# Quantised cross attention: the last two of six projection roundings moved from VectorE to ScalarE

## The reference

```python
def _fq(x, delta, zp, n_bits):
    xi = _round_ste(x / delta) + zp
    xq = jnp.clip(xi, 0.0, 2.0 ** n_bits - 1.0)
    return (xq - zp) * delta

def _attn(x, ctx, wq, wk, wv, wo, bo, dq, dk, dv, dw):
    q = (x @ wq).reshape(b, n, H, DH).transpose(0, 2, 1, 3)
    k = (ctx @ wk).reshape(b, m, H, DH).transpose(0, 2, 1, 3)
    v = (ctx @ wv).reshape(b, m, H, DH).transpose(0, 2, 1, 3)
    sim = einsum('bhid,bhjd->bhij', _fq(q, dq, 128.0, 8), _fq(k, dk, 128.0, 8)) * SCALE
    attn = jax.nn.softmax(sim, axis=-1)
    out = einsum('bhij,bhjd->bhid', _fq(attn, dw, 0.0, 8), _fq(v, dv, 128.0, 8))
    return out.transpose(0, 2, 1, 3).reshape(b, n, D) @ wo + bo
```

## Time and profile before

| | |
|---|---|
| median of 3 runs | 2308.91 us (2307.79 to 2310.9) |
| the profiled execution's own time | 2313.39 us |
| its span in the trace | 2311.7 us |
| PE / DVE / ACT / POOL busy, whole span | 1911.3 / 1630.2 / 1309.5 / 1001.5 us |
| mean granted TensorE clock, whole span | 0.912 of full |
| quantised cross attention, first to last instruction | about 1632 to 2247 us |

### The profile page before, as it was taken

How to read it: one execution, slowest core, us unless ns; L and a number is a source line. 1 busy time by engine, 2 the same in 40 slices (tenths; PEclk the granted TensorE clock), 3 DMA queues, 4 the chain that set the end, 5 groups by cost and what they waited for, 6 DMA issues and landing times. The chain is left out here.

```text
span 2311.7 us, 58368 instructions
## 1 busy us (share of the span) xinstructions
PE 1911.3 (83%) x20005; PEld 1291.4 (56%) x20005; DVE 1630.2 (71%) x2948; ACT 1309.5 (57%) x2351; POOL 1001.5 (43%) x1181
## 2 busy tenths in 40 slices
PE   4888666699999999999887777445699999999988
PEld 3887233266666666666533444223366666666653
DVE  4899597666666666666433224998499999999984
ACT  2555243366666676666533333222588888888863
POOL 2333162355455455445000000331488888888840
PEclk9999798799999999999888888555799999999999
DMA  7777000233333233333009991000111111111100
GB/s 195 247 242 234 9 1 0 64 84 94 86 86 98 82 88 98 85 94 88 21 11 282 266 256 37 0 0 0 54 42 40 40 40 40 46 47 40 40 1 16
DMA packets 64287, 190.37 MB, mean 82 GB/s; under 512 B 19886, under 2 KB 27295, under 8 KB 64223
## 3 DMA queue, kind: packets, MB, share of 16 engines
q1 hardware_dynamic: 59614, 164.95, 26.0%
q0 software_dynamic: 4608, 24.58, 2.7%
HBM read 127.13 MB, written 25.49 MB: 66 GB/s over the span
## 5 line engine op out<-in xcount | busy, mean ns | idle before, releaser
L1284 DVE TENSOR_REDUCE c_part<-c_mxp 128x1 f32<-128x500 f32 x672 | 428.8, 678 | 211.9 <-PE c_mxp L1164 211.7
L1232 ACT ACTIVATE c_e<-c_stp 125x896 f32<-125x896 f32 x384 | 349.3, 917 | 167.7 <-PE c_stp L1178 166.4
L1927 ACT ACTIVATE c_e<-c_sp,alpha 128x750 f32<-128x750 f32 x448 | 391.8, 886 | 78.3 <-PE c_sp L1872 78.0
L1164 PE MATMUL c_mxp<-c_kh,c_qb 128*128 128x500 f16 x672 | 254.5, 381 | 7.2 <-DVE c_part L1284 3.7
L1963 DVE TENSOR_SCALAR c_ph<-c_e,c_inv 128x1500 f16<-128x1500 f32 x224 | 259.8, 1160 | 0.1
L1949 DVE TENSOR_SCALAR c_pt<-c_tp 125x768 bf16<-125x768 f16 x448 | 243.2, 546 | 1.0 <-PE c_tp L1885 0.2
L1885 PE MATMUL c_tp<-ident_h,c_ph 128*128 128x128 f16 x2688 | 223.8, 219 | 21.9 <-DVE c_pt L1949 21.5
L1885 PEld LDWEIGHTS c_tp<-ident_h,c_ph 128*128 128x128 f16 x2688 | 177.2, 98 | 106.2 <-DVE c_pt L1949 57.7
L1872 PE MATMUL c_sp<-c_ki,c_qb 128*128 128x375 bf16 x896 | 218.7, 326 | 12.2 <-ACT c_e L1927 11.8
L1178 PE MATMUL c_stp<-c_qs,c_ks 103*128 103x224 f16 x1536 | 210.2, 259 | 2.5 <-ACT c_e L1232 2.5
L742 POOL TENSOR_TENSOR s_qb<-qi,mask_head_ 128x896 bf16<-128x896 f32 (+1 forms) x32 | 54.7, 1712 | 324.8 <-SPq L735 231.9
(11 more groups left out here) (276 smaller groups left out, 3723.3 us busy)
## 6 DMA issues: line engine op xcount, KB each, us to landing
c_ct<-ctx_turned SPq DMA_DIRECT2D x64, 750.0 KB
ctx_turned<-l_ct POOLq DMA_DIRECT2D x32, 750.0 KB, 4.1
c_ks<-c_kh SPq DMA_DIRECT2D x256, 93.8 KB
f_ct<-ctx_turned SPq DMA_DIRECT2D x32, 750.0 KB
l_cn<-in_ctx SPq DMA_DIRECT2D x32, 672.0 KB
f_cn<-in_ctx SPq DMA_DIRECT2D x32, 672.0 KB
c_ks<-c_kl SPq DMA_DIRECT2D x128, 93.8 KB
l_cn<-in_ctx SPq DMA_DIRECT2D x32, 78.0 KB
```

The source lines that it names most:

```text
L1164: pe.matmul(mxp[:, (PIECES * p + s) % 2, 0:500], qh[p][:, 128 * (s // 3):128 * (s // 3) + 128], kh[p][:, 500 * (s % 3):500 * (s % 3) + 500 ...
L1232: act.activation(e[:, j % (2 * GROUP), :].rearrange("p (a c) -> p a c", a=2), stp[0:KP, 2 * (j % 2):2 * (j % 2) + 2, 0:448], ACT.Exp, scal ...
L1284: dve.reduce_max(part[:, s // 3, s % 3:s % 3 + 1], mxp[:, (PIECES * p + s) % 2, 0:500], axis=AX.X).then_inc(piece_max, 1)
L1927: act.activation(e[t % E_BUFFERS][:, HALF * h:HALF * h + HALF] .rearrange("p (k c) -> p k c", k=2), sp_[:, 2 * h:2 * h + 2, 0:375], ACT.Ex ...
```

## The change

The table of indices that VectorE rounds becomes empty. ScalarE's loop then makes all six roundings, and VectorE's branch at L1987 never runs.

```diff
@@ -1763,7 +1763,7 @@
         WEIGH = {4: (0, 6), 6: (6, NJ)}
         TURN_LAG = 3
         E_BUFFERS = 4
-        ON_VECTOR = (4, 5)
+        ON_VECTOR = ()
         USED_BACK = [4 if t >= E_BUFFERS else NT if t == 3 else 3 for t in range(NT)]
         ct = pair("ct", [128, NK])
         ki = pair("ki", [128, NK], BF16)
```

## The result

The changed kernel takes 2293.8 us in the median of six runs (2288.55 to 2301.13), against 2309.23 us (2306.55 to 2310.9) for the kernel before. The ratio is 0.9936, with a 95% interval of 0.9921 to 0.9951: faster by 0.64%, or 15.4 us. The prediction had 2298.0 us, 10.9 us faster. One later execution of the kernel before took 5438 us at a granted clock of 0.344 and is in none of the comparisons.

A forecast was written before the change was run, and what follows sets the result against it. It took a ring of waits over several engines, not VectorE alone, as the bound. 31 batches by 0.40 us less 1.5 gave 10.9 us, so 2298.0 us from the median 2308.91, range 2276 to 2305.

The forecast's parts named there:

- the ring: Cycle of waits through POOL, VectorE and TensorE that sets the 18.43 us period; the fifth projection's rounding lies on it.
- Gain 0.40 us per period: TensorE's sixth projection no longer waits for VectorE's rounding of the fifth to empty the PSUM bank: 0.40 us per period.
- margin and schedule on ScalarE: ScalarE rounds the fifth projection from about 1962.2 to 1963.0, 0.3 us before TensorE is ready for the sixth.
- I take zero: VectorE's weights of tile 6 meet POOL's query spread; whichever starts first, POOL comes out within 0.1 us of today.
- The ring is closed: From sixth projection to weighing, whose eighth key tile releases POOL's conversion; one moved rounding lies on this path, for 0.40 us.
- Cost 1.5 us, once: Before the first batch's exponentials, the table load comes behind ScalarE's sixth rounding: 1.5 us once, bounds 0 to 3.
- The sum: 31 batches by 0.40 us less 1.5 at the start: 10.9 us faster, 2298.0 us from the median 2308.91.
- VectorE as the only bound: Rival: VectorE's time decides, both roundings count whole, 1.32 us per period, 39.4 us faster, 2269.5; chance 5%.
- The bank no freer: Rival: ScalarE's rounding ends as late as VectorE's did, only the start's cost remains, 2310.4 us; chance 10%.
- ScalarE as the ring: Rival: delayed exponentials of tile 6 hold up POOL's total, 9.6 us slower, 2318.5 us; chance 6%.
- POOL's chain shortening: Rival: VectorE's weights of tile 6 leave POOL's way, saving a further 0.68 us per period, 2277 us; chance 7%.
- The signs named: Trace signs: period 18.03 us, sixth projection without wait, POOL waiting near 0.9; wrong if the period is below 17.9.

The follow-up runs named there:

- fifth_only: Changed kernel, but only the fifth projection's rounding goes to ScalarE and the sixth stays on VectorE: 2291.5 us, ratio 0.9924 to the kernel before; period 17.963 us.
- weigh8_before: Kernel before, with eight instead of six key tiles weighed at tile 4: period 18.434 us, as in the kernel before.
- early_table: Changed kernel with a one-column exponential before the first rounding, so the table loads there: lead-in 76.4 us against 77.2, period 17.934 us.
- weigh8_after: Changed kernel with eight key tiles weighed at tile 4: period 17.866 us against the changed kernel's 17.933.

## Why the prediction was right, and where it was off

*The bound.* That VectorE, busiest by far, was not alone on the ring was right: its 1.32 us a period of freed time shortened the period by 0.50, and the two roundings count 0.47 and 0.04 by themselves. Had VectorE's time been the bound, each would count 0.25.

*"Gain 0.40 us per period."* TensorE's wait before the sixth projection went, as worked out; margin and schedule on ScalarE held, with the rounding at 0.04 us after the projection's end. Measured 0.50. One piece missing is that a projection which doesn't wait is itself shorter: 1.09 us for 1.14, and POOL's conversion came 1.63 us after its start (1944.87 to 1946.50) for 1.68 (1963.70 to 1965.38). That gives 0.05, in fifth_only too. The other is the next point. In fifth_only it is 0.02 (7.24 us for 7.26), and 0.40, 0.05 and 0.02 are the 0.47 measured.

*"I take zero" for VectorE's weights against POOL's spread.* VectorE comes first, 0.05 to 0.20 us ahead, and POOL's spread is stretched instead of VectorE's weights. From the conversion of the fifth projection to the total of tile 1 POOL took 7.26 us before (1946.95 to 1954.21). POOL's timelines of the two totals, first of the kernel before, then of the changed kernel:

```profile
1954.21 0.34 POOL L1840 TENSOR_SCALAR c_total<-c_half,delta 128x1 f32<-128x1 f32 x1
```

```profile
1935.78 0.34 POOL L1840 TENSOR_SCALAR c_total<-c_half,delta 128x1 f32<-128x1 f32 x1
...
1953.77 0.34 POOL L1840 TENSOR_SCALAR c_total<-c_half,delta 128x1 f32<-128x1 f32 x1
```

After, it took 7.15 in one step of the loop's two (1928.63 to 1935.78) and 7.27 in the other (1946.50 to 1953.77). That is 0.05 less on average, inside the 0.1 that the prediction left open. It agrees with the Trainium skill ("SBUF — State Buffer", SBUF: two separate sides), by which the shared port pair goes to whoever starts first.

*"The ring is closed" through the weighing.* This was half of it. The ring in the prediction had one closing link where there were two that fell together. It did no harm here because both had the moved rounding ahead of them, which the prediction had not looked at: that much was luck. As a statement on what to cut next it was wrong: weigh8_before was expected to gain 0.75 us a period and gained nothing. The wait of 0.93 us in the earlier trace rows named TensorE; the end of the conversion, 0.48 us behind VectorE's weights, named VectorE.

*"Cost 1.5 us, once."* Between the last projection's end and the first exponential the walk was right. ScalarE's timelines of the first exponential, first of the changed kernel, then of early_table:

```profile
1643.01 1.28 ACT L1927 ACT_TABLE_LOAD   x1
1644.31 0.89 ACT L1927 ACTIVATE c_e<-c_sp,alpha 128x750 f32<-128x750 f32 x1
```

```profile
1626.21 1.28 ACT L1920 ACT_TABLE_LOAD   x1 [1.51 <-PEq L88]
...
1648.60 0.88 ACT L1930 ACTIVATE c_e<-c_sp,alpha 128x750 f32<-128x750 f32 x1
```

The first exponential stands 23.61 us into the stage (1644.31 less 1620.70) where it stood 22.01 before (1654.29 less 1632.29): 1.6 later. With the table loaded early it stands 22.39 into it, 1.2 us sooner, and at the steady loop 0.8 of that is left. What the start costs at the steady loop is less than 1.5: the lead-in of the changed kernel is 0.9 longer than that of fifth_only (77.2 for 76.3), where the load is over before the scores arrive. The one load costs 1.28 us where it stands, and the next exponential begins at once behind it.

*The sum.* 31 × 0.40 − 1.5 = 10.9. Measured on the stage: 13.5 in 27 periods, 0.2 in the lead-in and 0.5 at the end: 14.3. By whole runs: 15.4. Two terms were mis-sized. The period's was too small by 0.10, which is 2.7 us over 27 periods. Outside these periods the sum has four batches of 0.40 less 1.5, which is 0.1, where 0.8 was measured; most of that 0.7 is the start, 1.5 in the sum and 0.9 by fifth_only.

*Rivals.* VectorE as the only bound: no, 0.50 for 1.32. The bank no freer: no, no wait is left before the sixth projection. ScalarE as the ring: no; its exponentials of tile 6 ended at 1946.18, and POOL took that total at 1947.11. (With eight key tiles weighed early, in weigh8_after, POOL does wait for them.) POOL's chain shortening: hardly, 0.05. The Trainium skill's rule that multiplies and adds belong on VectorE ("ScalarE: Activation LUTs", Rules for kernel authors) would have kept the roundings there. Here ScalarE's 96 value roundings average 779 ns and VectorE's 64 averaged 736, and the move away from VectorE was the faster.

*The signs named.* The period was to be 18.03 and came to 17.93, just above the 17.9 below which the prediction called itself wrong. The sixth projection has no wait, POOL waits 1.04 us for the weighing (near 0.9 expected) and ScalarE 0.24 for the first score (0.4 expected). VectorE's waits for totals and before the masking grew by about 40 us, where nearly 30 was expected. VectorE's busy time fell by 59.8 us in the whole span (1630.2 to 1570.4), where the roundings taken off it make 47. The groups by line show one source of the rest. VectorE's weights, in the kernel before and in the changed one:

```profile
L1963 DVE TENSOR_SCALAR c_ph<-c_e,c_inv 128x1500 f16<-128x1500 f32 x224 | 259.8, 1160 | 0.1
```

```profile
L1963 DVE TENSOR_SCALAR c_ph<-c_e,c_inv 128x1500 f16<-128x1500 f32 x224 | 229.1, 1023 | 0.1
```

And POOL's spread in the changed kernel:

```profile
L1831 POOL TENSOR_TENSOR c_qb<-qi,mask_head_ 128x896 bf16<-128x896 f32 x28 | 67.8, 2422 | 0.0
```

The weights lost 30.7 us without any change to them. The spread's mean went the other way, from the 1.69 us of the earlier trace rows to 2.42. What is booked as VectorE's work was in part time held up by POOL, and it changed sides. The 47 and the 30.7 don't add up to 59.8. A group in a stage that the change doesn't touch rose by 7.0 (L353, 53.0 to 60.0), and in the groups' sums the overlap of one instruction with the next counts twice.

## What to carry to other kernels

Follow the ring of waits round once, through every engine, before pricing an engine's time: of two equal instructions taken off the busiest engine, one was worth 0.47 us a period and the other 0.04. A wait's named releaser is only the last to come, and another may have come just before it; compare the end of the released instruction with what else was running. And when an expected number comes out, look whether it came by the expected way: in weigh8_after it did not. Then look at the other engines' stretches of the ring: here POOL's, where moving one instruction on the kernel before gave 0.58 us a period, more than the change's 0.50.

## What was not expected

Full attention, a stage well ahead of the one changed, took from 174.7 to 193.2 us from its first load to its last weighing over fourteen traces of the same code, which shifts all that follows: the start of the stage of the change lay between 1616.7 and 1632.3 us. I did not look for its cause.

A projection that has waited takes 1.14 us and one that has not takes 1.09, at a granted clock of 1.00 in both. It is so for all 25 sixth projections of the kernel before between 1710 and 2180 us, against the 50 fourth and fifth ones; in the changed kernel all take 1.09. I don't know why.

VectorE's weights and POOL's instructions hold each other up both ways, as seen in 0.99 against 2.17 us, 1.69 against 2.37 to 2.49, 0.62 against 1.39, and 0.34 against 1.02. At the conversion of the fifth projection 0.07 us decided for VectorE in weigh8_before and 0.03 for POOL in weigh8_after. What was moved away from one such meeting met the same partner at another place.
